# A two-dimensional Fourier block: x split into fp16 parts and transformed in pairs of 64-row tiles inside the first stage

## What is computed

```python
v = group_norm(x)                                  # per image, 32 groups
bias = v @ bias_w.T + bias_b
xf = rfftn(v.reshape(B, H, W, 4, 96), axes=(1, 2), norm='ortho')
r1 = relu(xr @ w1[0] - xi @ w1[1] + b1[0]);  i1 = relu(xr @ w1[1] + xi @ w1[0] + b1[1])
r2 = r1 @ w2[0] - i1 @ w2[1] + b2[0];        i2 = r2 @ w2[1] + i1 @ w2[0] + b2[1]
out = x + irfftn(complex(r2, i2), axes=(1, 2), norm='ortho') + bias
```

## Time and profile before

| | |
|---|---|
| median of 3 runs | 431.16 us (430.12 to 432.9) |
| the profiled execution: its own time, its span | 432.9 us, 431.1 us |
| PE busy, PE weight loads busy | 401.2 us (93%), 354.2 us (82%) |
| DVE, ACT, POOL busy | 283.1 us (66%), 228.9 us (53%), 84.1 us (19%) |
| chain that ended last | 90% of the span on PE |

### The profile page before, as it was taken

The page is one execution under the profiler, slowest core; times in us unless marked ns, Lnnn a source line. Parts: engine busy times, 40 slices in busy tenths (PEclk is TensorE's granted clock), DMA queues, the critical chain, the costliest instruction groups (busy, mean ns, idle before and its releaser), DMA issues.

```text
span 431.1 us, 19365 instructions
## 1 busy us (share of the span) xinstructions
PE 401.2 (93%) x8610; PEld 354.2 (82%) x8610; DVE 283.1 (66%) x696; ACT 228.9 (53%) x514; POOL 84.1 (19%) x72
## 2 busy tenths in 40 slices
PE   4468799999999999999999999999999999998996
PEld 4467689788898889887898889888898889986894
DVE  4697676864677656874668656865568646767425
ACT  2884865257742666356652576437662666426410
POOL 0000002700063000900036000810027000690000
PEclk9759999999999999999999999999999999999999
DMA  7670000270004300180003600161001700040004
GB/s 220 196 240 2 2 3 5 84 249 2 5 28 171 139 3 3 40 292 4 3 5 122 213 2 5 41 238 57 5 3 68 267 3 5 27 161 2 5 3 148
DMA packets 12406, 33.03 MB, mean 77 GB/s; under 512 B 4962, under 2 KB 6532, under 8 KB 12324
## 3 DMA queue, kind: packets, MB, share of 16 engines
q1 hardware_dynamic: 12324, 31.80, 21.0%
HBM read 16.07 MB, written 12.58 MB: 66 GB/s over the span
## 4 chain that ended last, share of the span: by engine, by line
PE 90%; ACT 4%; issue 2%; DVE 2%; DMA 1%; DVEq 0%; SPq 0%; ACTq 0%
PE bank L571 90%; DMA x_sb<-in_x 1%; ACT y L912 1%; ACT junk L900 1%; ACT yraw L892 1%; ACT r L922 1%; ACT biasw L926 1%; DVE o_sb L1114 0%; ACT w2s L926 0%; DVE r L1098 0%; ACT z L932 0%; ACT junk L903 0%; DVE rho L1029 0%; ACT rho L951 0%; DVE z L1029 0%
## 5 line engine op out<-in xcount | busy, mean ns | idle before, releaser
L571 PE MATMUL bank<-biasw,y 128*64 128x384 f16 x1152 | 111.1, 336 | 0.4 <-issue 0.4
L571 PEld LDWEIGHTS bank<-biasw,y 128*64 128x64 f16 x1152 | 93.4, 196 | 2.5 <-issue 1.0
L571 PE MATMUL bank<-w2s,rho 128*64 128x96 f16 x3072 | 84.9, 207 | 0.0
L571 PEld LDWEIGHTS bank<-w2s,rho 128*64 128x64 f16 x3072 | 80.0, 109 | 4.0 <-issue 2.5
L877 POOL TENSOR_TENSOR x_sb<-x_sb,added 128x384 f32<-128x384 f32 x56 | 74.8, 1370 | 0.0
L571 PE MATMUL bank<-w1R,y 128*128 128x192 f16 (+3 forms) x768 | 60.3, 228 | 5.9 <-ACT y L912 3.2
L1029 DVE SCALAR_TENSOR_TENSOR rho<-bank,rho 128x256 f16<-128x256 f32 (+2 forms) x128 | 39.9, 363 | 34.1 <-ACT rho L951 23.1
L932 ACT ACTIVATE z<-bank 128x384 f16<-128x384 f32 x72 | 35.3, 490 | 49.9 <-PE bank L571 48.9
L875 POOL TENSOR_TENSOR x_sb<-x_sb,added 128x384 f32<-128x384 f32 x8 | 8.1, 1009 | 270.5 <-DVE yraw L1085 270.5
L917 ACT ACTIVATE g<-bank 128x384 f16<-128x384 f32 x64 | 30.0, 480 | 53.4 <-PE bank L571 53.4
L571 PE MATMUL bank<-tab,x_sb 128*128 128x128 f32 x384 | 50.6, 287 | 7.7 <-DMA x_sb<-in_x 6.2
(11 more groups left out here) (109 smaller groups left out, 414.8 us busy)
## 6 DMA issues: line engine op xcount, KB each, us to landing
x_sb<-in_x SPq DMA_DIRECT2D x16, 768.0 KB, 6.7
out<-o_sb SPq DMA_DIRECT2D x14, 768.0 KB, 3.7
y<-y SPq DMA_DIRECT2D x24, 128.0 KB, 2.7
out<-o_sb SPq DMA_DIRECT2D x8, 192.0 KB, 1.9
tab<-in_tab SPq DMA_DIRECT2D x1, 672.0 KB, 5.6
o_sb<-in_bias_wt SPq DMA_DIRECT2D x4, 144.0 KB, 2.9
b1raw<-in_b1h SPq DMA_DIRECT2D x1, 384.0 KB, 5.9
tab<-in_tab SPq DMA_DIRECT2D x1, 292.5 KB, 3.0
```

Source lines behind the costliest of these rows:

```text
L571: return nc.tensor.matmul(o, lhsT, rhs, start=start, stop=stop, **kw)
```

## The change

What it does, part by part.

1. **The width transform of images 2 to 7 is fp16.** x is split into two fp16 parts (`x16`), scaled by a power of two per image. One item m is now 24 matmuls: four tiles t, three products of parts (high-high, high-low, low-high), two halves j of 64 rows, the halves into two different PSUM banks. The table is `widthx` (64 rows by 64 columns). Images 0 and 1 keep the fp32 form `p1`.
2. **It moves.** Item m stands right behind unit u = m + 2 of c1 of the image before. `p3_half(b, 0)` moves from before unit 6 to before unit 8. Nothing is left between p3_half(b, 1), p3_last and p4.
3. **The split.** ACT squares and sums x of image b + 2 (`x_square`, two halves, behind g_high(2) and g_high(3)), PE sums over partitions (`x_sum`, behind tile 5), DVE and ACT make the scale (`x_clamp`, `x_sqrt`, `x_scales`), ACT writes the high part (`x_high`, two halves, before g_high(7)), DVE the low part (`x_low`, two halves, behind z of units 0 and 2 of the next image's c1).
4. **Three x buffers, sums in place.** `add_x` writes into `x_sb`, the store reads `x_sb`, `o_sb` is gone. The load of image b + 3 waits for the store of image b.
5. **add_map** (POOL) starts once the low part of z of unit 0 of its own image is written.
6. **Group means** are one fp32 matmul in place of two; two more small DVE steps before each (`shared`).

The diff, cut to its core:

```diff
+        def p1_pair(m):
+            at = (5, 0)[m % 2]
+            return psum[:, at:at + 2, :].rearrange("k b (x c) -> k (b x) c", x=2)[:, :, 0:128]
...
+            def p1_rows(b, m):
+                h, ct = m // NT, m % NT
+                if m == 0:
+                    pe.wait_ge(gl_ready, 8 * b)
+                if m == 1:
+                    pe.wait_ge(o_ready, 8 * b)
+                    pe.wait_ge(dve_step, NSTEP * (b - 1) + VAR_READ)
+                if m >= 2:
+                    pe.wait_ge(y_raw, Y_ITEMS * b + m - 1)
+                if ct == 0:
+                    pe.wait_ge(xl_ready, 2 * (b - 2) + h + 1)
+                bank = p1_pair(m)
+                for i in range(4):
+                    t = 4 * h + i
+                    for of, w in ((0, 0), (0, 1), (1, 0)):
+                        for j in range(2):
+                            rows = slice(64 * j, 64 * j + 64)
+                            last = mm(bank[:, 2 * j:2 * j + 2, 32 * i:32 * i + 32], x16[rows, of, t, 128 * ct:128 * ct + 128],
+                                      widthx[rows, w, 0 if t == 0 else 1, :], of == 0 and w == 0, of == 1, skip_group_check=True)
+                last.then_inc(y_prod, 1)
...
-                mm(y_bank[0][:, at:at + NT], own, src[:, 0:NT], True, False)
-                return mm(y_bank[0][:, at:at + NT], block3, src[:, NT:NT + 1].to_broadcast([128, NT]), False, True)
+                return mm(y_bank[0][:, at:at + NT], groups, src[:, :], True, True)
...
-                    if u == 6:
-                        p3_half(b, 0, first)
+                    if u == (8 if more and not first else 6):
+                        p3_half(b, 0, more, first)
...
+                    if more and not first and 2 <= u < 8:
+                        p1_rows(b + 1, u - 2)
...
+                    if more and not first:
+                        pe.wait_ge(y_raw, Y_ITEMS * (b + 2))
...
-                    if more:
+                    if first:
                         p1(b + 1, 1 - p, m)
...
-                pool.wait_ge(dve_step, NSTEP * min(b + 2, BATCHES))
+                pool.wait_ge(rl_ready, 9) if b == 0 else pool.wait_ge(zl_ready, 9 * b + 1)
...
+                if split:
+                    x_high(b + 2, 0)
+                    x_high(b + 2, 1)
                 g_high(b, 7, more)
...
+            def x_low(b, h):
+                dve.wait_ge(xh_ready, 2 * (b - 2) + h + 1)
+                flat = "k t c -> k (t c)"
+                low(x16[:, 1, 4 * h:4 * h + 4, :].rearrange(flat), x_sb[b % 3][:, 4 * h:4 * h + 4, :].rearrange(flat), xscale[:, :],
+                    x16[:, 0, 4 * h:4 * h + 4, :].rearrange(flat)).then_inc(xl_ready, 1)
...
+                    if more and not first and u in (0, 2):
+                        x_low(b + 1, u // 2)
```

More of the change, by code:

```diff
@@ L185, in constants @@
     put("width", width.reshape(2, 128, 128).transpose(1, 0, 2))
+    lines = width.reshape(2, 2, 64, 2, 16, 2, 2)
+    assert not lines[:, 0, :, :, :, 1].any() and not lines[:, 1, :, :, :, 0].any()
+    lines = np.stack([lines[:, j, :, :, :, j] for j in range(2)])
+    put("widthx", H_SCALE * lines.transpose(0, 2, 1, 5, 3, 4).reshape(128, 128))
     put("height", P_SCALE * hgt.transpose(1, 0, 2))
@@ L192, in constants @@
     put("inv_low", G_EVAC * inv.astype(np.float16))
-    put("own", own)
-    put("block3", block3)
+    fourth = np.arange(128)[:, None] % 4 == 3
+    put("groups", own + block3)
+    put("fourth", np.concatenate([fourth, ~fourth], axis=1))
     put("const", np.broadcast_to(const, (128, 64)))
@@ L310, in spectral_block_kernel, with rho_bank @@
         c_bank = banks[5:8]
-        def rho_bank(j, more):
+        def rho_bank(j, more, first):
             if j < 6:
-                at = (2, 0 if more else 4)[j % 2]
+                at = ((0, 2) if more and not first else (2, 0) if more else (2, 4))[j % 2]
                 return psum[:, at:at + 2, :]
@@ L556, in _ @@
             block3_rows(0, 0)
+            sp.wait_ge(w2_forms, 12)
+            sp.wait_ge(bias_ready, 1 + NT)
+            load(2)
             for b in range(BATCHES - 2):
@@ L559, in _ @@
                 store(b)
-                load(b + 2, b % 2)
+                if b + 3 < BATCHES:
+                    load(b + 3)
             block3_rows(BATCHES - 1, 1)
@@ L609, in mm3, with c1 @@
                 return mm(o, S[1], W[0], False, stop, **kw)
-            def c1(b, p, first):
+            def c1(b, p, more, first):
                 pe.wait_ge(yh_ready, NT * b + 2)
@@ L661, in shift_product, with p3_half @@
                 last.then_inc(shift_prod, 1)
-            def p3_half(b, half, first):
+            def p3_half(b, half, more, first):
                 if half == 0:
@@ L713, in p4 @@
                             c2_bias(b, p, 3 - gi, more, first)
-                    if j == 0:
+                    if more and not first:
+                        if j == 1:
+                            pe.wait_ge(rl_ready, 9 * b + 6)
+                        elif 2 <= j < 6:
+                            pe.wait_ge(rhoh_ready, 8 * b + j - 1)
+                            pe.wait_ge(rhol_ready, 8 * b + j - 1)
+                        elif j == 7:
+                            pe.wait_ge(rhoh_ready, 8 * b + 6)
+                            pe.wait_ge(rhol_ready, 8 * b + 6)
+                    elif j == 0:
                         pe.wait_ge(rl_ready, 9 * b + 6)
@@ L734, in p4 @@
                         pe.wait_ge(rl_ready, 9 * b + (4, 8, 9)[j // 3])
-                    bank = rho_bank(j, more)
+                    bank = rho_bank(j, more, first)
                     if j < 6:
@@ L808, in image @@
             def image(b, p, more=True, first=False):
-                c1(b, p, first)
+                c1(b, p, more, first)
                 for m in range(Y_ITEMS):
-                    if more:
+                    if first:
                         p1(b + 1, 1 - p, m)
                     if m == 0:
-                        p3_half(b, 1, first)
+                        p3_half(b, 1, more, first)
                     if m == 2:
@@ L831, in image @@
                         variance(b + 1)
+                    if gi == 5 and b + 2 < BATCHES:
+                        x_sum(b + 2)
                 p6(b, range(EARLY, TILES))
@@ L932, in image @@
                     nc.scalar.activation(z[:, 0, u, :], b_bank[u % 3][:, 0:CH], ACT.Copy, scale=Z_EVAC).then_inc(zh_ready, 1)
-                    for v in {5: (0, 1), 6: (2,), 7: (3,)}.get(u, ()):
+                    if more and not first and 2 <= u < 8:
+                        y_copy_rows(b + 1, u - 2)
+                    for v in ({7: (0, 1), 8: (2, 3)} if more and not first else {5: (0, 1), 6: (2,), 7: (3,)}).get(u, ()):
                         r_high(b, v)
                 for m in range(Y_ITEMS):
-                    if more:
+                    if first:
                         y_copy(b + 1, m)
```

156 lines of the change are left out of this document (116 added, 40 removed).

## The result

The changed kernel takes 436.54 us (median, 434.7 to 437.65) beside 431.5 us for the kernel before on the same chip: a ratio of 1.0108, 95% interval 1.0076 to 1.014. It is slower by about one per cent. The profiled execution took 436.34 us with a span of 434.5 us.

The account below looks back on a forecast made before the run. PE's stream was taken as the bound: its work changes by -2.96 us an image, new waits add 3.1, so +0.14, times six +0.8 us on the 431.16 us median: 432.0 us, range 423 to 440.

Parts of the forecast that it names:

- Rival B: POOL's additions reach SBUF before x_low(0), making it 2.86 us, all awaited: +6.2 us, 438.2 us; chance 0.13.
- Rival C: Turns between tile shapes dear (0.70 us a visit) or PE's stream pauses grow: up to 441.5 us; chance 0.07.
- Rival D: The 64-row halves don't run side by side, so 24 matmuls take 0.8 us: +14 us, 446 us; chance 0.04.
- stream pauses: PE pauses up to 1.52 us that wait for nothing the trace shows; effect -2.7 to +3 us, taken as 0.
- six visits: Items between c1's units: 0.40 us for 24 matmuls plus 0.12 for turns, 0.52 a visit, 3.12 us an image.
- (a): In c1, PE's item 0 waits for DVE's x_low(0): 1.12 us an image.
- (b): p3_half(b, 0) waits for ACT's last yraw copy, whose banks items 4 and 5 used: 0.85 us an image.
- (c): p3_half(b, 1) waits for half 0's second relu part, 1.7 us, of which unit 8 covers about 1.0: 0.65 us.
- (d): Around p3_last and inside p4, PE waits for DVE's relu parts of units 4 to 8: net 0.5 us an image.
- Rival A: Visits cost only their slots, 0.36 us: 5.8 us less, 426.2 us, or 423 with less waiting for x_low(0); chance 0.28.
- What lies beside: ACT's added squares and high parts fit, 0.4 us left before g_high(7); faster y_low worth nothing; shared buffers' loads used an image later.
- The turn rule: Weight loads overlap matmuls in flight only where row groups differ, so each full-array/half turn exposes a load; upper bound 0.70 a visit.

Follow-up runs that it names:

- e8: Changed kernel with the items' form and place of the kernel before, the low parts of x left out; ratio 0.9958 to the kernel before, 430.7 us.
- e1: Changed kernel with items 0 to 3 one unit later and items 4 and 5 both behind unit 7; 433.5 us, ratio 1.0046 to the kernel before.
- e2: Changed kernel with items 4 and 5 both behind unit 6; 430.9 us, ratio 0.9992 to the kernel before.
- e7: Changed kernel with the low part of x made earlier, in four operations of 768 elements; 433.1 us, ratio 1.0033 to the kernel before.
- e4: Changed kernel with POOL's additions again starting after the next image's statistics; 439.0 us, ratio 1.0181 to the kernel before.
- e6: Changed kernel with items in their new places and banks but the old fp32 form; 444.0 us, ratio 1.0261 to the kernel before.
- e3: Changed kernel with items in four visits, not six: 0 behind unit 3, 1-2 behind 4, 3-4 behind 5, 5 behind 6; 426.7 us, ratio 0.9893.

## Why the prediction came out as it did

The forecast was no change, 432.0 us, with a range of 423 to 440. The measured 436.5 us lies in the range. The ratio's 1.08% is just past the 1% that I had set for "no change", so it falls among the outcomes that I had called slower (0.24), and none of the three rivals that stood for them (B, C, D) is what happened. One of my own signs of being wrong came true: the image moved by 1.08 us, where 0.7 was the bound. The kinds and the places of the waits were right: what leaves PE's stream comes back as waits, from the engines named. The size was not: +0.14 us an image predicted, +1.08 measured. That the time stayed 3.5 us inside the range is in part luck: stream pauses, which I took at 0, gave 1.9 us back in the profiled execution.

Term by term, from the rows above and the earlier trace rows, and for unit 8 from these two pieces of PE's order of time, the kernel before (no pause in this image):

```profile
340.33 0.42 PE L571 MATMUL bank<-w1R,y 128*128 128x192 f16 x3
...
342.42 0.72 PE L571 MATMUL bank<-w1R,y 128*32 128x96 f16 x48
343.07 1.16 PE L571 MATMUL bank<-tab,x_sb 128*128 128x128 f32 x8
```

| term, us an image | predicted | measured |
|---|---|---|
| fp32 items gone | -5.90 | -5.90 |
| group means, x_sum | -0.18 | about 0 (e8: an image is 49.00 against 48.99) |
| six visits | +3.12 | 6 x 0.565 = +3.39 |
| (a) wait for x_low(0) | +1.12 | 4.22 - 2.97 = 1.25, less 0.11 that is in the visit = +1.14 |
| (b) wait for the copy | +0.85 | 1.37 - 0.565 = +0.81 |
| (c) wait for the relu parts | +0.65 | unit 8 and the wait 302.72 - 300.97 = 1.75, unit 8 before 343.07 - 342.42 = 0.65: +1.10 |
| turn between units 7 and 8, gone | no term | 342.42 - 340.33 = 2.09, two units 1.98: -0.11 |
| (d) waits in p3_last and p4 | +0.5 | +0.64: from p3_half(b, 1) to c2_rho(0) 313.94 - 302.72 = 11.22, without the items 10.58 before |
| sum | +0.14 | +1.07, of 1.08 |

- *What bounds the kernel*: right. e1, e2 and e7 each took a wait away and the image followed. (The clock is at the upper level from the fourth slice on, not the fifth.)
- *The waits*: (c) is the term that was furthest off. The chain behind it was right: 1.7 us from the end of p3_half(b, 0) to DVE's second relu part, and PE started again after 1.75. "Unit 8 covers about 1.0 of it" had no row, and unit 8 covers 0.65 to 0.71 us. (a) and (b) came out within 0.04 us. (d) was low by 0.14.
- *The visit*: the step "0.12 us over the 0.40" was mis-sized. A visit has 0.36 us of slots and 0.20 of turns; I had let one of the two turns hide in p4's 0.40. Rival A, visits that cost only their slots, falls.
- *The means*: each takes 0.31 us now (267.33 to 267.64) and so does x_sum, as put down. But the 48 c2_rho matmuls ahead of such a small fp32 matmul take 1.12 us and not 1.02, so x_sum costs 0.41, and what the means save goes for it.
- So the 0.93 us between forecast and measurement are +0.34 in (c) and its turn, +0.27 in the visits, +0.18 in the means, +0.14 in (d), all on one side.
- *What lies beside*: right for what e8 holds: squares, high parts, buffers and sums in place cost nothing. ACT's cover before g_high(7) was as thin as stated; e4 shows what happens when it goes.
- *Rival B, POOL first*: it did not come. x_low(0) took 1.81 us beside POOL's first addition, which took 2.51 us: DVE was first and POOL waited. By the Trainium skill's rule ("SBUF — State Buffer", Who interferes with whom) an operation of this kind is not lengthened as long as it is first; the trace agrees. x_low(1), with the addition first, took 2.58 us. That is over the 2.5 I had named as a sign of being wrong, but nobody awaits it.
- *The turn rule*: turns between the full array and 64-row tiles cost 0.20 us a visit; an fp32 item on the full array in the same place costs at most 0.07 over its matmuls (e6). The Trainium skill's sentence that a load overlaps matmuls in flight only where its row group differs ("TensorE: Matmul & The Clock Gate", Part 3) agrees in that turns have a price. Taken by its words it would also lay open each load in c1, where full-array matmuls follow each other, and the trace does not agree: 12 of them, each with its load, take 0.99 us, 82 ns each, while one such load has 100 ns in the trace. That exposed loads are what makes the turn cost is not shown.
- *Rival C*: its stream pauses did not grow here, they shrank (between 65 and 390 us the changed kernel's chain has none over 0.2 us). *Rival D*: 24 matmuls in 0.36 us, so the pairs do run side by side.

## What to carry to other kernels

Where an engine's stream is full, moving work to a cheaper form is worth its price difference only if what the old form covered is still covered: list, for each wait that the old place hid, how long the chain behind it takes and which piece of the bound engine's work will stand over it. Take the length of that piece from its own row, too: the largest error here was a unit of 0.65 us put at 1.0. The same cheap form is slower by 1.1% in one order and faster by 1.1% in another (e3), and only which unit each item follows differs. Change between tile shapes as seldom as possible: put small visits together. Compare images by the distance in the trace, beside the medians: the clock and the stream pauses move a median by as much as the effects here.

## What was new about the hardware

- A visit of 64-row tiles between full-array matmuls costs 0.20 us in turns, once for 24 or for 48 matmuls; an fp32 visit on the full array costs at most 0.07 us beyond its matmuls (0.92 us for four in e6, 0.85 to 0.89 for four more in the earlier trace rows).
- PE's granted clock fell to the lower level inside a steady stretch in some runs of some variants: in e1 from 150 to 156 us, 2.1 us lost. What decides it was not tested.
- ACT's copy of 512 columns took 687 ns in the new form, which reads from two banks with one dimension more and scales by a tile, and 604 ns in the old form, in the same kernel. In e6, with one bank and without the scale in the same place, it took 597 ns. Pattern and scale were not told apart:

```profile
L978 ACT ACTIVATE yraw<-bank,xunscale 128x512 f32<-128x512 f32 x36 | 24.7, 687 | 8.1 <-PE bank L607 7.1
...
L970 ACT ACTIVATE yraw<-bank 128x512 f32<-128x512 f32 x12 | 7.1, 604 | 5.0 <-PE bank L607 5.0
```

- PE's stream pauses did not grow with the matmuls in the stream: 2.7 us in three images before, about 0.8 us in the changed kernel, which has 556 matmul records more, 2.5 us in e3, which has the same matmuls in another order. What brings them on was not tested.
